# The masked operands of the inverse's levels one to four, made by GpSimd instead of VectorE

## Chip, cores and metric

The kernel runs on one core of a Trainium2 chip. The metric is the device time of one execution in microseconds, the median over several executions. TensorE is PE, its weight loads PEld, VectorE DVE, ScalarE ACT, GpSimd POOL, SyncE SP.

## What is computed

Two sequences of 2048 tokens with 256 channels are normalised. One branch is a recurrent layer (RWKV7 form) with four heads of 64, the other an attention layer with a mixture of four experts; the output is x plus the product of the two. What matters here is the recurrence, a state of 64 x 64 for each sequence and head:

```python
def step(S, inp):
    rt, dt, kt, vt, kkt, at = inp
    sa = jnp.einsum('bhvk,bhk->bhv', S, -kkt)
    S = S * dt[:, :, None, :] + sa[..., None] * (kkt * at)[:, :, None, :] + vt[..., None] * kt[:, :, None, :]
    y = jnp.einsum('bhvk,bhk->bhv', S, rt)
    return (S, y)
...
x = x + s * g          # s: this layer's output; g: silu of the attention and experts branch
```

## The kernel before, in words

Three phases run one after the other: the recurrent phase (up to about 1170 us), the attention, the experts. Only the recurrent phase is touched.

It takes 16 turns t of 128 tokens of both sequences. The steps of the recurrence are done by chunks of 64 tokens (CH), so a turn has 4 chunks of 2 halves of the channels: 8 pairs (PAIRS), each with two heads stacked on the 128 partitions. Within a chunk the feedback through `sa` is a triangular system of 64 x 64, and the kernel inverts it by doubling: `inv` and `invT` start as the inverse of blocks of two (the masks of `base`), and five further levels (`lev` 0 to 4; LEVELS is 6) join blocks of twice the size. A level needs the part of the matrix below its diagonal blocks: `am[:, :, 0, :]`, the first of seven products kept for each pair, times a 0/1 mask `lev`. That is the masked operand `lj`, held in two buffers `lj[0]` and `lj[1]` in turns. Of a level, PE first makes z = inv x lj into bank 4, ACT copies it to `zz`, PE makes invT x zz and zz x invT into banks 5 and 6, and DVE adds these to `inv` and `invT`. At the last level only `invT` is updated.

Each engine's program of a turn interleaves three strands: `back(t)`, the inverse and the chunks of turn t; `front(t)`, the projections and features of the next 128 tokens; `tail(t - 1)`, the group norm and output projection of the turn before. `back` calls `give_way()` at fixed places, and each call runs the other two strands up to their next `yield`. So the order on each engine is fixed by the code; an engine does its rows in order, and the engines meet only in semaphores. A `Signal` counts the steps of a turn: `at(t, n)` is the value at which n of turn t are done. The first turn has no tail and the last no front.

On DVE the row of work at the start of a turn is: r_yc of the tail, the statistics of the next x, eight masked products `am` (L870), after the fourth and after the eighth the five masks of `base` (L857 to L863) on half the pairs, and then the front's dx (L731) and token mixes (L709), whose g is PE's next input (g1). Before the change DVE makes `lj` of level 0 in `base` (L860) and that of levels 1 to 4 at L880, each at the head of the level before its use, ahead of the front and tail work that `give_way` brings. PE waits for `s_lj`, which counts six signals a turn: two of `base`, four of L880. GpSimd has no program in this phase.

Of the kernel before, what the change touches and what calls it, by code (L numbers as in the profile page):

```python
# [8 lines left out]
ALU = mybir.AluOpType  # L9
# [8 lines left out]
NT = T // TT  # L18
# [3 lines left out]
PAIRS = CB * HALVES  # L22
LEVELS = int(math.log2(CH))
# [62 lines left out]
def all_strands(eng, front, back, tail):  # L86


    for _ in front(FIRST):
        pass  # L90

    def turn(t, before, after):
        strands = [tail(t - 1) if before else iter(()), front(t) if after else iter(())]

        def give_way():
            for strand in strands:
                next(strand, None)

        back(t, give_way)
        for strand in strands:  # L100
            for _ in strand:
                raise AssertionError("the strands differ in length")

    turn(0, False, True)
    with eng.Fori(1, NT - 1) as t:
        turn(t, True, True)
    turn(NT - 1, True, False)
    for _ in tail(NT - 1):
        pass


def recurrent_phase(nc, io, keep, signal):
# [13 lines left out]
    with ctx:  # L126
        def sb(name, shape, dt=FP32):
            return ctx.enter_context(nc.sbuf_tensor("r_" + name, shape, dt))

        def sig(name, per, unit=1):  # L130
            return signal("r_" + name, per, unit)
# [8 lines left out]
        def v(name, h):  # L140
            return vec[:, VECS.index(name), h:h + 1]
# [34 lines left out]
        am = sb("am", [128, PAIRS, 7, 64])  # L176
        inv, invT, zz = (sb(n, [128, PAIRS, 64]) for n in ("inv", "invT", "zz"))
        lj = [sb(f"lj{i}", [128, PAIRS, 64]) for i in range(2)]
# [25 lines left out]
        def by_batch(ap):  # L204
# [10 lines left out]
        s_adec, s_vst = sig("a_r_decayed", 1), sig("v_stacked", 1)  # L215
        s_xsq, s_h, s_hsq, s_cut = sig("xn_squared", 1), sig("h", 1), sig("qk_squared", 2), sig("parts", 2)
        s_am, s_amsb = sig("products", PAIRS), sig("products_kept", PAIRS)
        s_lj, (s_z, s_zsb, s_inv, s_invsb) = sig("level_off", LEVELS), (sig(n, LEVELS - 1) for n in (
            "z", "z_kept", "inverse_step", "inverse_kept"))
        s_g, s_gsb, s_u, s_usb, s_sn, s_state, s_y, s_ysb = (sig(n, NCH) for n in (  # L220
            "chunk_g", "chunk_g_kept", "chunk_u", "chunk_u_kept", "state_gain", "state", "chunk_y", "chunk_y_kept"))
# [3 lines left out]
        front_step, back_step, tail_step = sig("dve_front_step", 15), sig("dve_back_step", 5), sig("dve_tail_step", 2)  # L225
        s_base = sig("transposed_base", 2)
# [5 lines left out]
        block = ctx.enter_context(nc.Block())  # L232
# [53 lines left out]
        def _(pe):  # L286
            back_signals, tail_signals = (s_am, s_z, s_inv, s_g, s_u, s_sn, s_y), (s_mean, s_gvar, s_out)
# [117 lines left out]
            def back(t, give_way):  # L405
# [24 lines left out]
                def pairwise(bk, left, right):  # L430
                    apart()
                    for p in range(PAIRS):
                        for j in range(2):
                            q = slice(64 * j, 64 * j + 64)
                            last = mm(ps[q, bk, 64 * p:64 * p + 64], left[q, p, :], right[q, p, :], start=True, stop=True)  # L435
                    return last

                for lev in range(LEVELS - 1):
                    if lev:
                        pe.wait_ge(s_invsb.sem, s_invsb.at(t, lev))  # L440
                    pe.wait_ge(s_lj.sem, s_lj.at(t, lev + 2))
                    pairwise(4, lj[lev % 2], inv).then_inc(s_z.sem, s_z.up())
                    give_way()
                    pe.wait_ge(s_zsb.sem, s_zsb.at(t, lev + 1))
                    if lev == 0:
                        pe.wait_ge(s_base.sem, s_base.at(t, 2))
                    if lev < LEVELS - 2:
                        pairwise(5, invT, zz)
                    pairwise(6, zz, invT).then_inc(s_inv.sem, s_inv.up())
                    give_way()  # L450
# [231 lines left out]

        @block.vector
        def _(dve):
            back_signals = (s_amsb, s_base, s_lj, s_invsb, s_state, back_step)
            tail_signals = (s_yc, s_yg, tail_step)
            for q in back_signals + tail_signals:
                q.open(dve)
# [1 line left out]
            ve = nc.vector  # L690
# [157 lines left out]
            def back(t, give_way):  # L848
                flat = lambda a: a[:, :, :].rearrange("p a c -> p (a c)")
                wide = lambda name, lo=0, hi=64, n=PAIRS: const(name, lo, hi).unsqueeze(1).to_broadcast([128, n, 64])  # L850

                def base(p):


                    n = PAIRS // 2
                    dve.wait_ge(s_amsb.sem, s_amsb.at(t))
                    ve.tensor_tensor(inv[:, p, :], am[:, p, 6, :], wide("low0", n=n), ALU.mult)  # L857
                    ve.tensor_tensor(invT[:, p, :], am[:, p, 0, :], wide("low0t", n=n), ALU.mult
                                     ).then_inc(back_step.sem, back_step.up())
                    ve.tensor_tensor(lj[0][:, p, :], am[:, p, 0, :], wide("lev", 0, 64, n), ALU.mult)  # L860
                    dve.wait_ge(back_step.sem, back_step.at(t))
                    ve.tensor_tensor(inv[:, p, :], inv[:, p, :], wide("eye64", n=n), ALU.add).then_inc(s_lj.sem, s_lj.up())  # L862
                    ve.tensor_tensor(invT[:, p, :], invT[:, p, :], wide("eye64", n=n), ALU.add  # L863
                                     ).then_inc(s_base.sem, s_base.up())


                give_way()
                for p in range(PAIRS):
                    dve.wait_ge(s_am.sem, s_am.at(t, p + 1))
                    ve.tensor_tensor(am[:, p, :, :].rearrange("p a c -> p (a c)"), ps[:, 4 + p % 3, 0:448],  # L870
                                     const("amask"), ALU.mult).then_inc(s_amsb.sem, s_amsb.up())
                    if p == PAIRS // 2 - 1:
                        base(slice(0, PAIRS // 2))
                        give_way()
                base(slice(PAIRS // 2, PAIRS))
                dve.wait_ge(s_base.sem, s_base.at(t))
                give_way()
                for lev in range(LEVELS - 1):
                    if lev < LEVELS - 2:
                        ve.tensor_tensor(lj[(lev + 1) % 2][:, :, :], am[:, :, 0, :], wide("lev", 64 * lev + 64, 64 * lev + 128),  # L880
                                         ALU.mult).then_inc(s_lj.sem, s_lj.up())
                    give_way()
                    dve.wait_ge(s_inv.sem, s_inv.at(t, lev + 1))
                    if lev < LEVELS - 2:
                        ve.tensor_tensor(flat(inv), flat(inv), ps[:, 5, :], ALU.add)  # L885
                    ve.tensor_tensor(flat(invT), flat(invT), ps[:, 6, :], ALU.add).then_inc(s_invsb.sem, s_invsb.up())
                    dve.wait_ge(s_invsb.sem, s_invsb.at(t))
                    if lev == 2:


                        for h in range(2):
                            ve.tensor_scalar(gain[:, h, :], gT[:, h, :], v("ln_w", h), None, ALU.mult)
                            last = ve.scalar_tensor_tensor(shift[:, h, :], bonus[:, h, :], v("ln_b", h), gT[:, h, :],
                                                           ALU.add, ALU.mult)
                        last.then_inc(back_step.sem, back_step.up())
                        dve.wait_ge(back_step.sem, back_step.at(t))
                    give_way()
                for c in range(NCH):
                    fl = lambda a: a[:, :, :, :].rearrange("p b g v -> p (b g v)")
                    give_way()  # L900
                    give_way()

                    dve.wait_ge(s_sn.sem, s_sn.at(t, c + 1))
                    ve.tensor_tensor(fl(stmp), fl(state), ps[:, 6, 0:256], ALU.add).then_inc(back_step.sem, back_step.up())
                    dve.wait_ge(back_step.sem, back_step.at(t))
                    ve.tensor_tensor(state[:, :, :, :], stmp[:, :, :, :],
                                     p_end[:, c, :, :].unsqueeze(3).to_broadcast([128, B, 2, 64]), ALU.mult
                                     ).then_inc(s_state.sem, s_state.up())
                    dve.wait_ge(s_state.sem, s_state.at(t))
                    give_way()  # L910
                back_step.whole()
                for q in back_signals:
                    q.restart()
# [22 lines left out]
                    q.restart()  # L936

            all_strands(dve, front, back, tail)


PARTS_Q, PARTS_K = (0, 0, 0, 1, 1, 2), (0, 1, 2, 0, 1, 0)
# [957 lines left out]
```

## Time and profile before

| what | value |
|---|---|
| median of 3 runs | 3104.87 us (3094.93 to 3106.5) |
| the profiled execution | 3108.72 us, span 3106.9 us |
| PE busy | 2727.6 us, 88% |
| DVE busy | 2074.6 us, 67% |
| ACT busy | 1330.4 us, 43% |
| POOL busy | 63.7 us, 2%, x91 |

The span runs from the first to the last instruction of the profiled execution. Busy shares are means over three phases with different limits; what the change is worth has to be read from the waits and the timeline of the recurrent phase. A number in square brackets behind an instruction is the idle time of its engine before it and the instruction that ended it. A tile's name carries r_ in front for this phase; `cst` holds the masks, `xn_all` the normalised input. A row with x4 or x32 is a run of equal instructions merged, its time that of the whole run.

### The profile page before, as it was taken

What the parts mean: (1) busy time and instruction counts of PE and PEld (TensorE: products, weight loads), DVE (VectorE), ACT (ScalarE), POOL (GpSimd) and SP (SyncE); (2) the same over time, 40 slices, a digit from 0 to 9 for tenths busy, and PEclk for the clock granted to TensorE, in tenths of its full rate; (3) what the DMA queues carried; (4) which work ended last, traced back from release to release, by engine and by line L of the source; (5) the groups of instructions that cost most, each with busy time, mean ns of one, the idle gap of its engine ahead of it and who ended that gap; (6) DMA issues with size and microseconds to landing.
All of it is one profiled execution on the core that took longest, in us unless ns stands there. A gap on an engine that the chain in (4) does not pass through costs nothing. (4 is left out here: it accounts for less than half of the span.)

```text
span 3106.9 us, 71943 instructions
## 1 busy us (share of the span) xinstructions
PE 2727.6 (88%) x27049; PEld 1834.5 (59%) x27049; DVE 2074.6 (67%) x4070; ACT 1330.4 (43%) x1993; POOL 63.7 (2%) x91
## 2 busy tenths in 40 slices
PE   6988888888888876898988989889894999999999
PEld 5767776767777761233323323232333999999999
DVE  6666766776666748776776767667674555655654
ACT  3333333333333410155555555545552554445444
POOL 0000000000000001000000000000004000000000
PEclk9999999999999985699999999999997999999999
DMA  2000000000100003001111010110104010011010
GB/s 65 19 19 19 21 24 23 20 19 19 26 19 19 16 16 98 1 21 36 32 36 45 12 45 23 44 46 11 45 21 132 28 34 27 24 34 32 22 30 24
DMA packets 141929, 96.89 MB, mean 31 GB/s; under 512 B 69088, under 2 KB 137312, under 8 KB 140640
## 3 DMA queue, kind: packets, MB, share of 16 engines
q1 hardware_dynamic: 140064, 87.66, 9.8%
q0 software_dynamic: 1600, 5.24, 0.5%
q8 instruction: 221, 3.62, 0.5%
q14 instruction: 44, 0.36, 0.0%
HBM read 63.18 MB, written 29.36 MB: 30 GB/s over the span
## 5 line engine op out<-in xcount | busy, mean ns | idle before, releaser
L1209 DVE TENSOR_REDUCE a_mx<-a_pm 128x1 f32<-128x512 f32 (+3 forms) x1440 | 812.6, 607 | 280.8 <-PE a_pm L1091 147.0
L1192 ACT ACTIVATE a_pt<-a_sc 128x1024 f32<-128x1024 f32 (+3 forms) x640 | 562.0, 896 | 611.8 <-PE a_sc L1120 426.8
L1088 PE MATMUL a_pm<-a_ka,a_qa 96*128 96x512 bf16 (+3 forms) x1440 | 521.2, 379 | 98.5 <-DVE a_mx L1209 56.5
L1088 PEld LDWEIGHTS a_pm<-a_ka,a_qa 96*128 96x128 bf16 x1440 | 136.4, 98 | 582.3 <-DVE a_mx L1209 511.2
L1120 PE MATMUL a_sc<-a_qa,a_ka 98*128 98x512 bf16 (+3 forms) x1280 | 368.5, 361 | 37.4 <-DMA a_qa<-a_mrow 33.2
L1167 PE MATMUL a_po<-a_pt,a_v_st 128*32 128x512 f32 (+3 forms) x2560 | 305.2, 549 | 0.0
L1759 DVE TENSOR_TENSOR e_h_lo<-v_all,e_h_hi 128x512 fp32r<-128x512 f32 x208 | 145.7, 701 | 189.1 <-ACT e_h_hi L1606 187.9
L1120 PEld LDWEIGHTS a_sc<-a_qa,a_ka 98*128 98x128 bf16 x1280 | 116.7, 100 | 147.5 <-issue 50.3
L1604 ACT ACTIVATE v_all<-e_ps 128x512 f32<-128x512 f32 x176 | 103.6, 589 | 124.2 <-PE e_ps L1496 123.4
L1496 PE MATMUL e_ps<-e_h_hi,e_e_l_hi 128*128 128x256 f32 x512 | 147.7, 288 | 0.0
L1496 PE MATMUL e_ps<-e_h_lo,e_e_l_hi 128*128 128x256 f32 x512 | 144.8, 283 | 0.0
L1496 PE MATMUL e_ps<-e_h_hi,e_e_l_lo 128*128 128x256 f32 x512 | 144.8, 283 | 0.0
L885 DVE TENSOR_TENSOR r_inv<-r_inv,r_ps 128x512 f32<-128x512 f32 x64 | 43.9, 686 | 132.3 <-PE r_ps L435 132.3
L1091 PE MATMUL a_pm<-a_masks 128*128 128x128 bf16 x576 | 131.1, 235 | 0.0
L435 PE MATMUL r_ps<-r_zz,r_invT 64*64 64x64 f32 x2048 | 83.4, 238 | 46.9 <-ACT r_zz L645 46.9
L435 PE MATMUL r_ps<-r_inv,r_lj 64*64 64x64 f32 x2560 | 95.7, 226 | 32.1 <-DVE r_inv L862 27.6
L435 PEld LDWEIGHTS r_ps<-r_inv,r_lj 64*64 64x64 f32 x2560 | 85.0, 139 | 55.9 <-issue 55.9
L435 PEld LDWEIGHTS r_ps<-r_zz,r_invT 64*64 64x64 f32 x2048 | 74.6, 151 | 71.3 <-issue 71.3
L1606 ACT ACTIVATE e_h_hi<-v_all 128x512 fp32r<-128x512 f32 x176 | 111.1, 631 | 5.7
L645 ACT ACTIVATE r_zz<-r_ps 128x512 f32<-128x512 f32 x80 | 47.3, 591 | 141.3 <-PE r_ps L435 141.3
L1123 PE MATMUL a_sc<-a_masks 128*128 128x128 bf16 x512 | 101.4, 219 | 0.0
L1496 PEld LDWEIGHTS e_ps<-e_h_lo,e_e_l_hi 128*128 128x128 f32 x512 | 98.2, 192 | 0.4
(321 smaller groups left out, 5627.4 us busy)
## 6 DMA issues: line engine op xcount, KB each, us to landing
a_qa<-q_scratch SPq DMA_DIRECT2D x240, 64.0 KB, 2.3
a_ka<-k_scratch SPq DMA_DIRECT2D x240, 64.0 KB, 2.3
o_scratch<-a_o_sb SPq DMA_DIRECT2D x8, 1024.0 KB, 5.6
v_all<-o_scratch SPq DMA_DIRECT2D x256, 32.0 KB
q_scratch<-r_q_part SPq DMA_DIRECT2D x192, 32.0 KB, 1.8
k_scratch<-r_k_part SPq DMA_DIRECT2D x192, 32.0 KB, 1.6
r_x_tok<-in_x SPq DMA_DIRECT2D x32, 128.0 KB, 2.1
s_scratch<-r_s_tok SPq DMA_DIRECT2D x32, 128.0 KB, 1.7
```

What stands on the lines that cost most here:

```text
L435: last = mm(ps[q, bk, 64 * p:64 * p + 64], left[q, p, :], right[q, p, :], start=True, stop=True)
L1088: last = mm(out[:, 0:width], qa[b][0:NP, h, 128 * qt:128 * qt + 128], ka[b][0:NP, h, 512 * kc:512 * kc + width], start=True, stop=not diag)
L1091: last = mm(out[:, width - 128:width], ident16, neg_qk, start=False, stop=True)
L1120: last = mm(sc[x][:, y, off:512], ka[b][:, h, 128 * j:128 * j + 128], qa[b][:, h, 512 * qc + off:512 * qc + 512], start=True, stop=not diag)
L1123: last = mm(sc[x][:, y, off:off + 128], ident16, neg_kq, start=False, stop=True)
L1167: last = mm(po[qc % 2][32 * h:32 * h + 32, off:512], v_st[b][:, j, h, :], pt[h // 2][n % 2][:, h % 2, off:512], start=(j == 0), stop=(j == ...
L1192: nc.scalar.activation(pt[x][n % 2][:, :, off:512], sc[x][:, :, off:512], ACT.Exp).then_inc(s_p[x].sem, s_p[x].up())
L1209: return ve.tensor_reduce(mx[:, h, qt, kc:kc + 1], pm[i % 2][:, 0:width], axis=AX.X, op=ALU.max)
L1496: last = mm(out, a, b, start=(n == 0), stop=(n == len(products) - 1))
L1604: f(tmp[m % 2][:, :, :], two, ACT.Gelu).then_inc(by["A"].sem, by["A"].up())
L1606: f(hi[dst][:, o:o + 2, :], tmp[m % 2][:, :, :], ACT.Copy).then_inc(s_hi.sem, s_hi.up())
L1759: ve.tensor_tensor(lo[dst][:, o:o + 2, :], tmp[m % 2][:, :, :], hi[dst][:, o:o + 2, :], ALU.subtract).then_inc(s_lo.sem, s_lo.up())
```

## The change

The four products that make `lj` for levels 1 to 4 leave DVE's program, and GpSimd gets a program of its own in this phase that makes them: level 1 when all eight products `am` of the turn are kept, each further level when PE has done the first product of the level before the one in hand (`s_z`), which frees the buffer. `lj` of level 0 stays with DVE. PE waits for a signal of its own for level 0 (`s_first`) and for GpSimd's (`s_lj`) at the others.

```diff
-        s_lj, (s_z, s_zsb, s_inv, s_invsb) = sig("level_off", LEVELS), (sig(n, LEVELS - 1) for n in (
+        s_first, s_lj, (s_z, s_zsb, s_inv, s_invsb) = sig("base", 2), sig("level_off", LEVELS - 2), (sig(n, LEVELS - 1) for n in (
             "z", "z_kept", "inverse_step", "inverse_kept"))
@@ PE
-                    pe.wait_ge(s_lj.sem, s_lj.at(t, lev + 2))
+                    if lev:
+                        pe.wait_ge(s_lj.sem, s_lj.at(t, lev))
+                    else:
+                        pe.wait_ge(s_first.sem, s_first.at(t, 2))
                     pairwise(4, lj[lev % 2], inv).then_inc(s_z.sem, s_z.up())
@@ DVE, base
-                    ve.tensor_tensor(inv[:, p, :], inv[:, p, :], wide("eye64", n=n), ALU.add).then_inc(s_lj.sem, s_lj.up())
+                    ve.tensor_tensor(inv[:, p, :], inv[:, p, :], wide("eye64", n=n), ALU.add).then_inc(s_first.sem, s_first.up())
@@ DVE, levels
                 for lev in range(LEVELS - 1):
-                    if lev < LEVELS - 2:
-                        ve.tensor_tensor(lj[(lev + 1) % 2][:, :, :], am[:, :, 0, :], wide("lev", 64 * lev + 64, 64 * lev + 128),
-                                         ALU.mult).then_inc(s_lj.sem, s_lj.up())
                     give_way()
@@ new
+        @block.gpsimd
+        def _(pool):
+            s_lj.open(pool)
+
+            def levels(t):
+
+                pool.wait_ge(s_amsb.sem, s_amsb.at(t, PAIRS))
+                for lev in range(LEVELS - 2):
+                    if lev:
+                        pool.wait_ge(s_z.sem, s_z.at(t, lev))
+                    mask = const("lev", 64 * lev + 64, 64 * lev + 128).unsqueeze(1).to_broadcast([128, PAIRS, 64])
+                    nc.gpsimd.tensor_tensor(lj[(lev + 1) % 2][:, :, :], am[:, :, 0, :], mask, ALU.mult
+                                            ).then_inc(s_lj.sem, s_lj.up())
+                s_lj.restart()
+
+            levels(0)
+            with pool.Fori(1, NT - 1) as t:
+                levels(t)
+            levels(NT - 1)
```

On DVE, at the places that the text calls A and B, from the first mask of `base` on the second half of the pairs in the first turn, the row was, before:

```order
L857 TENSOR_TENSOR r_inv<-r_am,cst 128x256
L858 TENSOR_TENSOR r_invT<-r_am,cst 128x256
L860 TENSOR_TENSOR r_lj0<-r_am,cst 128x256
L862 TENSOR_TENSOR r_inv<-r_inv,cst 128x256
L863 TENSOR_TENSOR r_invT<-r_invT,cst 128x256
L731 TENSOR_TENSOR r_dx<-xn_all 128x512
L709 SCALAR_TENSOR_TENSOR r_xg<-r_dx,vec,xn_all 128x256 x2
L709 SCALAR_TENSOR_TENSOR r_xw<-r_dx,vec,xn_all 128x256 x2
L880 TENSOR_TENSOR r_lj1<-r_am,cst 128x512
L709 SCALAR_TENSOR_TENSOR r_xa<-r_dx,vec,xn_all 128x256 x2
```

And after the change (the same instructions have line numbers higher by three):

```order
L860 TENSOR_TENSOR r_inv<-r_am,cst 128x256
L861 TENSOR_TENSOR r_invT<-r_am,cst 128x256
L863 TENSOR_TENSOR r_lj0<-r_am,cst 128x256
L865 TENSOR_TENSOR r_inv<-r_inv,cst 128x256
L866 TENSOR_TENSOR r_invT<-r_invT,cst 128x256
L734 TENSOR_TENSOR r_dx<-xn_all 128x512
L712 SCALAR_TENSOR_TENSOR r_xg<-r_dx,vec,xn_all 128x256 x2
L712 SCALAR_TENSOR_TENSOR r_xw<-r_dx,vec,xn_all 128x256 x2
L712 SCALAR_TENSOR_TENSOR r_xa<-r_dx,vec,xn_all 128x256 x2
```

Only L880's row is gone; everything else keeps its place. On GpSimd, the loop's turn now is (before, this engine had no row in the phase):

```order
L951 TENSOR_TENSOR r_lj1<-r_am,cst 128x512 [waits r_products_kept]
L949 ISA
L951 TENSOR_TENSOR r_lj0<-r_am,cst 128x512 [waits r_z]
L949 REGISTER_ALU
L951 TENSOR_TENSOR r_lj1<-r_am,cst 128x512 [waits r_z]
L949 REGISTER_ALU
L951 TENSOR_TENSOR r_lj0<-r_am,cst 128x512 [waits r_z]
```

Each of the four products has a wait of its own: the first on the event that also lets DVE's masks go, the others on PE's first product of the level before.

## Rows read from the trace of the kernel before

**Rows 1.** First line; then 100 us: PE, PEld, DVE, ACT, POOL busy, granted clock, DMA.
```profile
span 3106.9 us, 71943 instructions
...
600.00:700.00 100.00, 84.91 (x1322) 69.18 (x1318) 72.92 (x159) 34.23 (x68) 0.00 (x0) 1.00 0.10 23
```

**Rows 2.** Waits from 71 to 1140 us: total us, times, longest.
```profile
PE r_ps L435 <- DVE r_inv L862: 25.9, 15, 2.3
...
PE r_ps L313 <- DVE r_xg L709: 12.5, 14, 1.1
```

**Rows 3.** Timeline, turn 8, all engines: start, us, engine, line, operation, idle before.
```profile
619.07 0.42 DVE L857 TENSOR_TENSOR r_inv<-r_am,cst 128x256 f32<-128x256 f32 x1
...
620.09 0.42 DVE L862 TENSOR_TENSOR r_inv<-r_inv,cst 128x256 f32<-128x256 f32 x1
...
620.65 1.15 PE L435 MATMUL r_ps<-r_inv,r_lj 64*64 64x64 f32 x32 [1.69 <-DVE r_inv L862]
621.12 0.69 DVE L731 TENSOR_TENSOR r_dx<-xn_all 128x512 f32 x1 [0.29 <-DVE r_invT L863]
...
621.85 0.88 DVE L709 SCALAR_TENSOR_TENSOR r_xg<-r_dx,vec,xn_all 128x256 f32<-128x256 f32 x2
...
622.87 1.13 PE L313 MATMUL r_ps<-r_xg,r_g 128*128 128x256 f32 x4 [1.07 <-DVE r_xg L709]
623.44 0.69 DVE L880 TENSOR_TENSOR r_lj<-r_am,cst 128x512 f32<-128x512 f32 x1
```

**Rows 4.** The tile r_lj: count, duration in ns (min/median/max).
```profile
L880 DVE TENSOR_TENSOR r_lj<-r_am,cst x64: 680/685/693, 64.4 to 1135.4; 128x512 f32<-128x512 f32 x64
```

**Rows 5.** The same timeline further on, DVE and PE.
```profile
631.62 0.68 DVE L926 TENSOR_TENSOR r_yg<-r_yc,r_ystd 128x512 f32<-128x512 f32 x1
...
633.07 0.69 DVE L930 TENSOR_TENSOR r_yg<-r_yg,r_shift 128x512 f32<-128x512 f32 x1
...
634.02 1.99 PE L520 MATMUL r_ps<-r_W_o,r_yg 128*128 128x256 f32 x8
```

**Rows 6.** Timeline of DVE from 640 us.
```profile
645.78 0.69 DVE L885 TENSOR_TENSOR r_inv<-r_inv,r_ps 128x512 f32<-128x512 f32 x1 [2.22 <-PE r_ps L435]
...
650.04 0.68 DVE L880 TENSOR_TENSOR r_lj<-r_am,cst 128x512 f32<-128x512 f32 x1
```

**Rows 7.** Timeline of PE from 640 us.
```profile
653.58 1.15 PE L435 MATMUL r_ps<-r_zz,r_invT 64*64 64x64 f32 x32 [2.92 <-ACT r_zz L645]
```

**Rows 8.** Line L1301, GpSimd products of two SBUF operands: durations in ns.
```profile
L1301 POOL TENSOR_TENSOR e_l_lo<-a_stage,e_l_hi x2: 1256/1256/1256, 1221.8 to 1224.6; 128x512 fp32r<-128x512 f32 x2
```

**Rows 9.** Timeline from 2377.6 us: DVE back to back, then beside a GpSimd product.
```profile
2377.71 0.69 DVE L1790 TENSOR_TENSOR e_e_down_lo<-v_all,e_e_down_hi 128x512 fp32r<-128x512 f32 x1 [1.29 <-ACT e_e_down_hi L1618]
2378.32 0.69 DVE L1790 TENSOR_TENSOR e_e_l_lo<-v_all,e_e_l_hi 128x512 fp32r<-128x512 f32 x1
...
2379.56 1.58 POOL L1301 TENSOR_TENSOR e_e_l_lo<-v_all,e_e_l_hi 128x512 fp32r<-128x512 f32 x1
...
2379.95 2.35 DVE L1790 TENSOR_TENSOR e_e_l_lo<-v_all,e_e_l_hi 128x512 fp32r<-128x512 f32 x2
...
2381.62 0.68 DVE L1790 TENSOR_TENSOR e_e_l_lo<-v_all,e_e_l_hi 128x512 fp32r<-128x512 f32 x1
```

**Rows 10.** Timeline of DVE: r_yc (L918) opens each turn; four of them.
```profile
116.71 0.69 DVE L918 SCALAR_TENSOR_TENSOR r_yc<-r_ps,r_yT 128x512 f32<-128x512 f32 x1 [0.22 <-PE r_ps L507]
...
609.82 0.69 DVE L918 SCALAR_TENSOR_TENSOR r_yc<-r_ps,r_yT 128x512 f32<-128x512 f32 x1 [1.99 <-PE r_ps L507]
...
678.02 0.69 DVE L918 SCALAR_TENSOR_TENSOR r_yc<-r_ps,r_yT 128x512 f32<-128x512 f32 x1 [1.94 <-PE r_ps L507]
...
1102.93 0.69 DVE L918 SCALAR_TENSOR_TENSOR r_yc<-r_ps,r_yT 128x512 f32<-128x512 f32 x1 [0.21 <-PE r_ps L507]
```

**Rows 11.** Timeline of PE: the g1 group in two other turns.
```profile
129.61 1.80 PE L313 MATMUL r_ps<-r_xg,r_g 128*128 128x256 f32 x4 [1.08 <-DVE r_xg L709]
...
978.75 2.07 PE L313 MATMUL r_ps<-r_xg,r_g 128*128 128x256 f32 x4 [0.25 <-DVE r_xg L709]
```

More of the change, by code:

```diff
@@ L684, in _ @@
         def _(dve):
-            back_signals = (s_amsb, s_base, s_lj, s_invsb, s_state, back_step)
+            back_signals = (s_amsb, s_base, s_first, s_invsb, s_state, back_step)
             tail_signals = (s_yc, s_yg, tail_step)
```

## The prediction

> **What bounds the kernel now.** I read the busy time first, then the waits of TensorE (PE), then the timeline around each wait. In a stretch of 100 us in the recurrent phase PE is busy 84.91 us and VectorE (DVE) 72.92 us, and GpSimd (POOL) does nothing [rows 1]. So DVE's busy time is not the limit by itself: what it does costs time only where PE, or somebody PE waits for, stands behind it. The operand that moves, r_lj, never makes PE wait. The waits of PE that name DVE in this phase are 25.9 us on r_inv from L862 (15 times) and 12.5 us on the mixed operand r_xg from L709 (14 times) [rows 2]. Both lie within four microseconds at the start of the inverse, once in each turn. In turn 8 DVE ends the last of eight products r_am at about 619.0, starts the base masks at 619.07, and starts L862 at 620.09; PE, idle for 1.69 us, starts the first product r_ps<-r_inv,r_lj at 620.65. It is idle again for 1.07 us until r_xg is there, and starts the g1 projection at 622.87 [rows 3]. I call these places A and B. From 622.87 the timeline shows PE occupied almost without a break until it waits 2.92 us, up to 653.58, for ScalarE's r_zz [rows 7]; I call that C. The chain to C begins with PE itself: DVE waits 2.22 us for PE's products at 645.78, updates the inverse, and some steps later hands ScalarE the norms that its row of work before r_zz needs.
>
> **What is removed, and what it is worth.** DVE loses four products a turn, 64 in all, 685 ns each [rows 4], 64 x 0.685 = 43.8 us of busy time. I look at what follows each of them.
> Level 1 (623.44) stands behind r_xg and r_xw, so A and B end before it [rows 3]. What follows it are r_xa and r_xk, which PE reaches only behind g1, w1 and the second half of the level before: worth nothing.
> Level 2 stands ahead of the three products that make r_yg for the output projection. From its start, 631.01, to the start of the next, 631.62, are 0.61 us; r_yg ends at 633.07 + 0.69 = 633.76, and PE's L520 starts at 634.02 directly behind its group before [rows 5]. r_yg was already in time by 0.26 us: worth nothing.
> Level 3 is followed by DVE's wait for PE of 2.22 us [rows 6]: worth nothing.
> Level 4 (650.04) comes after the norm that ScalarE waits for, and in front of a step that waits for ScalarE [rows 6]: worth nothing to C.
> So the work removed is hidden today by PE's own work, and if that cover were gone a level would be worth 0.61 us.
>
> **What is added.** GpSimd makes the same four products. No row shows it doing so in this phase. The nearest rows are its products of two SBUF operands of 128x512 further on, 1256 ns with nothing beside them [rows 8]; I take 1.26 us. Here one operand is read in eight pieces of 64 and the other is repeated eight times. If GpSimd has to be told of each piece, it might be twice that, 2.5 us, which I take as the upper bound; the lower is DVE's own 0.685 us. The result is in time in either case: level 1 is made after the eighth r_am and read after PE's whole row of groups from 622.87, and each later level is made one level ahead.
>
> What it costs others is the point. The row to look at is where GpSimd's product runs beside DVE products of two SBUF operands. Back to back these start 0.61 us apart, at 2377.71 and 2378.32. One that starts at 2379.95, while GpSimd's is under way from 2379.56 for 1.58 us, holds its successor off until 2381.62, so 1.67 us: 1.06 us lost, and the DVE product ends about when GpSimd's has ended plus its own work [rows 9]. GpSimd's product is itself longer than 1.26 by 0.32. They take turns. The base masks (L857 to L863), r_dx (L731) and the mixes (L709) all read two operands in SBUF; the updates of the inverse and r_am read one of theirs from PSUM, and I take these as free of it.
> The Trainium skill speaks against the change here: "SBUF — State Buffer", section "Who interferes with whom", says that a DVE instruction with two SBUF inputs and a GpSimd one that reads SBUF exclude each other for the whole instruction. By that rule each meeting would cost the full 1.26 us and the sum below would be 45 us without the clock, where the row gives 36. The same skill's "GPSIMD Engine Reference", section "Elementwise — side-by-side cycle accounting", has 4497 ns for 2048 elements; a quarter is an estimate of 1.12 us, and with 0.92 lost at a meeting the sum would be about 31 us.
>
> **The sum.**
> A: GpSimd's level 1 is released by the eighth r_am, the very event that releases DVE's five masks from 619.07. Even if DVE starts first, GpSimd comes between two of the five, and L862 is the fourth. 1.06 us later r_inv, and PE waits 2.75 instead of 1.69: 16 turns x 1.06 = 17.0 us.
> B: level 2 is released by PE's first product, which ends 1.15 us after its start, when DVE is at the two halves of r_xg (before: 620.65 + 1.15 = 621.80, and r_xg from 621.85 [rows 3]; both move by the same 1.06). One half waits again, or, if GpSimd is a little late, r_xw, which PE wants next. I take the full price: 15 turns with a next block of inputs x 1.06 = 15.9 us; the other bound is 0.
> Level 3 is released when PE's second level product ends, about 631.0, as DVE starts r_yg, now 0.61 us earlier. 1.06 - 0.61 = 0.45 late, less 0.26 in hand: 0.19 x 15 = 2.9 us.
> Level 4 falls before DVE's idle 2.22 us, which has grown by 0.61: nothing.
> PE does not make up what A and B cost, since C hangs on PE's own products. Together 17.0 + 15.9 + 2.9 = 35.8 us.
> The clock: in turn 8 the g1 group takes 1.13 us at the high level; in 8 of the 14 turns that follow the first it takes 1.7 to 2.07, the first and last being those at 129.61 and 978.75 [rows 3, 11], so TensorE was granted 1.2 instead of 2.4 GHz there, each time behind the idle time at A. The price of all such stretches, C's too: the 14 turns from 116.71 to 1102.93 take 70.44 us on average, turn 8 without one 678.02 - 609.82 = 68.20 [rows 10], so 2.24 x 14 = 31.4 us. With twice the idle time at A and B I expect the low level in all 15 turns, 7 more. If A's turns carry all of that price it is 31.4 / 8 = 3.9 each, 27 us; but the longer idle time itself covers part of a slow stretch, in the 8 turns too, so the lower bound is 0. I take 5, nearer the low end for that reason.
> Sum: 35.8 + 5 = about 41 us. The profiled execution took 3108.7 us (span 3106.9), the median of the runs is 3104.9, so it stands 3.9 above. On the median: **about 3146 us**, 1.3% slower.
>
> **Rivals.** A measurement tells 0.5%, 15.5 us, from no change.
> First, only one of the two meetings costs PE, because GpSimd starts late enough to fall in DVE's wait of 0.29 us before r_dx, or behind r_xg: one time 17 us, 3122. For it: no row shows how soon GpSimd starts after another engine's signal. Against: DVE's products stand without a gap for 1.8 us there.
> Second, no change: DVE and GpSimd run side by side here and the 64 products were hidden anyway: 3105. For it: the rows of the meeting are few and from another phase. Against: it is the same kind of instruction, same size.
> Third, faster: the delay at A moves the turn's idle times, and the stretches at the low clock become rarer. If they vanished, the stage would go to 68.20 a turn, 31 us less: 3074. It decides if at least half of the slow stretches go (15.7 us) while the meetings cost nothing; against it, more idle time stands ahead of the place where the clock is low already.
> Fourth, GpSimd's product takes 2.5 us: a meeting costs 2.5 - 0.2 = 2.3, so A 36.8, B 34.5, level 3 (2.3 - 0.61 - 0.26) x 15 = 21.5, together 93, 3198.
>
> **How the numbers follow.** Forecast 0.66 (its own range 3128 to 3166: from two thirds of the 35.8 with no clock term to all of it with 25 for the clock), first rival 0.13, no change 0.10, faster 0.05, fourth 0.06. A range from 3112 to 3182 leaves out the second and third rivals and most of the fourth, 0.2. Slower by over 0.5%: the forecast, the fourth and 0.09 of the first, 0.81; within 0.5%: 0.10 and the other 0.04, 0.14; faster 0.05.
>
> **What would show it.** In the changed profile: POOL products r_lj of about 1.26 us, some longer by 0.3; a mask of L860 to L865 and an r_xg that take near 1.5 us instead of 0.42; PE's wait on r_inv about 2.75 and on r_xg about 2.1; nothing waits for r_lj; g1 at the low clock in nearly all turns; later phases as before. It would be wrong if the masks keep 0.42 us, or if PE's waits at A and B are unchanged.

## The result, and the profile after

The changed kernel takes 3133.62 us (median of 4 runs, 3123.18 to 3143.25), beside 3104.73 us before in the same comparison: 1.0099 times the time, 95% interval 1.006 to 1.0138. It is 28.9 us slower; the forecast was 41 slower. The profiled execution is the shortest of the four, 3123.18 us, so its trace has about half of the median's loss in it.

The busy time of the changed kernel in a stretch of 100 us, with the columns of [rows 1]:

```profile
600.00:700.00 100.00, 87.02 (x1404) 71.18 (x1404) 70.46 (x147) 35.47 (x71) 6.17 (x4) 0.97 0.10 23
```

GpSimd is busy 6.17 us there and the granted clock is 0.97 of full speed, where [rows 1] show 0 and 1.00.

The waits of PE from 71 to 1140 us (total us, times, longest), to be held against [rows 2]:

```profile
PE r_ps L435 <- DVE r_inv L865: 42.0, 15, 3.4
...
PE r_ps L313 <- DVE r_xg L712: 3.5, 14, 0.3
PEld r_ps L523 <- DVE r_yg L930: 2.9, 14, 0.2
```

The wait on r_inv has grown from 25.9 to 42.0 us, and the wait on r_xg has shrunk from 12.5 to 3.5. A wait of the weight loads on r_yg is new, 2.9 us in 14 turns. Nothing in this list waits for r_lj.

The timeline of the changed kernel at places A and B in one turn, which answers to [rows 3]:

```profile
631.00 0.42 DVE L860 TENSOR_TENSOR r_inv<-r_am,cst 128x256 f32<-128x256 f32 x1
...
631.04 1.51 POOL L951 TENSOR_TENSOR r_lj<-r_am,cst 128x512 f32<-128x512 f32 x1 [45.80 <-DVE r_am L873]
631.34 1.49 DVE L861 TENSOR_TENSOR r_invT<-r_am,cst 128x256 f32<-128x256 f32 x1
...
633.65 1.98 PE L435 MATMUL r_ps<-r_inv,r_lj 64*64 64x64 f32 x32 [2.76 <-DVE r_inv L865]
...
634.85 0.88 DVE L712 SCALAR_TENSOR_TENSOR r_xg<-r_dx,vec,xn_all 128x256 f32<-128x256 f32 x2
635.65 1.89 DVE L712 SCALAR_TENSOR_TENSOR r_xw<-r_dx,vec,xn_all 128x256 f32<-128x256 f32 x2
...
635.70 1.55 POOL L951 TENSOR_TENSOR r_lj<-r_am,cst 128x512 f32<-128x512 f32 x1 [3.15 <-PE r_ps L435]
...
635.86 2.07 PE L313 MATMUL r_ps<-r_xg,r_g 128*128 128x256 f32 x4 [0.24 <-DVE r_xg L712]
```

The first mask and GpSimd's level 1 start 0.04 us apart, on the same event. The second mask, L861, takes 1.49 us where it took 0.42. PE waits 2.76 us, and its first product r_ps<-r_inv,r_lj takes 1.98 us in place of 1.15: the clock is low. So GpSimd's level 2, released by that product, starts at 635.70, when both halves of r_xg (from 634.85) are done, and it meets r_xw, 1.89 us for two halves in place of 0.88. PE starts g1 after a wait of 0.24 us.

GpSimd's products as a group (ns, minimum/median/maximum), to be held against [rows 4, 8]:

```profile
L951 POOL TENSOR_TENSOR r_lj<-r_am,cst x64: 1265/1508/1724, 60.9 to 1148.1; 128x512 f32<-128x512 f32 x64
```

It takes 1.26 or 1.27 us in three of the four products of the last turn, and 1.40 to 1.72 in all full turns, where a VectorE product of two SBUF operands is under way when it starts. 1.27 is the time of a product of plain rows [rows 8], so the eight strided pieces and the repeated mask cost nothing.

The same timeline at r_yg, which answers to [rows 5]:

```profile
645.71 0.69 DVE L926 TENSOR_TENSOR r_yg<-r_yc,r_ystd 128x512 f32<-128x512 f32 x1
...
645.82 1.72 POOL L951 TENSOR_TENSOR r_lj<-r_am,cst 128x512 f32<-128x512 f32 x1 [8.57 <-PE r_ps L435]
646.44 1.64 DVE L928 TENSOR_TENSOR r_yg<-r_yg,r_gain 128x512 f32<-128x512 f32 x1
...
648.11 0.69 DVE L930 TENSOR_TENSOR r_yg<-r_yg,r_shift 128x512 f32<-128x512 f32 x1
```

The second of the three products that make r_yg, L928, takes 1.64 us (1.64 or 1.65 in each of the 14 turns), and the three end 3.09 us after their start, beside 2.14 before.

The first and the last full turn, by r_yc, as in [rows 10]:

```profile
120.30 0.69 DVE L918 SCALAR_TENSOR_TENSOR r_yc<-r_ps,r_yT 128x512 f32<-128x512 f32 x1 [0.23 <-PE r_ps L510]
...
1120.93 0.69 DVE L918 SCALAR_TENSOR_TENSOR r_yc<-r_ps,r_yT 128x512 f32<-128x512 f32 x1 [0.21 <-PE r_ps L510]
```

1120.93 - 120.30 = 1000.63 us for 14 turns, 71.47 a turn, where the kernel before had 70.44.

### The profile page after: what moved, and what is told of

The parts are those of the page before. It is cut to its first block and busy times, and to the rows that moved or that the text cites. A ratio compares the mean times of both kernels' runs of the same rounds, so it can differ in the third digit from the quotient of the medians.

```text
span 3121.3 us, 72087 instructions
## 1 busy us (share of the span) xinstructions
PE 2736.2 (88%) x27049; PEld 1836.5 (59%) x27049; DVE 2099.0 (67%) x4006; ACT 1330.7 (43%) x1993; POOL 161.4 (5%) x155
## 5 line engine op out<-in xcount | busy, mean ns | idle before, releaser
L951 POOL TENSOR_TENSOR r_lj<-r_am,cst 128x512 f32<-128x512 f32 x64 | 97.5, 1524 | 1051.4 <-DVE r_am L873 736.1
L435 PE MATMUL r_ps<-r_inv,r_lj 64*64 64x64 f32 x2560 | 105.0, 240 | 49.4 <-DVE r_inv L865 44.7
L435 PEld LDWEIGHTS r_ps<-r_inv,r_lj 64*64 64x64 f32 x2560 | 93.8, 152 | 73.2 <-issue 73.2
L435 PE MATMUL r_ps<-r_zz,r_invT 64*64 64x64 f32 x2048 | 76.4, 226 | 46.8 <-ACT r_zz L648 46.8
L435 PEld LDWEIGHTS r_ps<-r_zz,r_invT 64*64 64x64 f32 x2048 | 68.0, 139 | 72.9 <-issue 72.9
```

## Experiments

Each was compared with runs of the kernel before on the same chip. There were three such groups: the first four experiments, beside 3099.2 us; B by itself, the VectorE delay, and the changed kernel and the kernel before with TensorE kept busy, beside 3101.8; and the other three, beside 3102.9. The theory is that of the prediction: what is saved is hidden, and GpSimd's reading holds VectorE off at A and B. The first rival: the loss lies elsewhere, in lost VectorE time or in the new signals.

### Nobody makes the operands

```diff
-                    pairwise(4, lj[lev % 2], inv).then_inc(s_z.sem, s_z.up())
+                    pairwise(4, lj[0], inv).then_inc(s_z.sem, s_z.up())
...
-        @block.gpsimd
```

> Nobody makes the masked operands of levels 1 to 4: VectorE's four products are gone and GpSimd has no program; every level reads the operand of level 0, so the output is not the reference's. It measures what the removal alone is worth. My theory (removed work is hidden by TensorE's own work): no change against the kernel before, 3105 within 8 us; TensorE's wait on r_inv at place A stays 1.69 us and the wait of 2.92 us at C stays. Rival (the saved VectorE work is worth something and the meetings at A ate it): 64 x 0.61 us at most, down to 3066, some 10 us faster or more.

Measured: 3096.3 us, 0.9986 (0.997 to 1.0002). Its waits of PE:

```profile
PE r_ps L435 <- ACT r_zz L646: 46.0, 18, 2.9
...
PE r_ps L435 <- DVE r_inv L863: 25.9, 15, 2.3
```

The wait on r_inv is the 25.9 us of [rows 2], and C's 2.9 is there. 43.8 us of VectorE's work removed give back 2.8 us in the median and at most 0.3%, 9 us, by the interval, which also reaches no change. The removed work was hidden. (The output is not the reference's, since every level reads the operand of level 0.)

### GpSimd's products added, VectorE's kept

```diff
+        def _(pool):
...
+                    nc.gpsimd.tensor_tensor(kT[:, :, :, :].rearrange("p h c d -> p (h c) d"), am[:, :, 0, :], mask, ALU.mult).then_inc(s_spare.sem, s_spare.up())
```

> The kernel before, with VectorE still making every masked operand, and GpSimd making the same four products a turn besides, at the same moments as in the changed kernel, into a buffer that is unused at that time. My theory (the cost is GpSimd's reading beside VectorE's products): as the changed kernel or a little more, 3125 to 3150, with the second mask of base at about 1.5 us instead of 0.42 and the wait on r_inv at 2.76. Rival (the cost is in how PE's waits and the two signals are arranged, not in GpSimd's reading): 3105.

Measured: 3146.0 us, 1.0137 (1.0109 to 1.0165). Its waits:

```profile
PE r_ps L435 <- DVE r_inv L864: 38.6, 14, 2.8
...
PE r_ps L313 <- DVE r_xg L709: 13.1, 14, 2.1
...
PE r_ps L520 <- DVE r_yg L932: 11.2, 14, 0.8
```

The cost comes with GpSimd's products; TensorE's signals are those of before (VectorE has one more wait a turn, before it writes the buffer that GpSimd uses). At 46.9 us it is 18 larger than in the changed kernel, and two waits say why. VectorE still has 0.61 us a level in front of r_yg, which now makes PE itself wait 11.2 us. And the wait on r_xg is 13.1 us in place of 3.5: in 5 of the 14 full turns PE's first product runs at 1.15 to 1.30 us though the wait in front of it was 2.76, and PE waits 1.93 to 2.08 us at B as well. In one of them:

```profile
571.81 1.15 PE L435 MATMUL r_ps<-r_inv,r_lj 64*64 64x64 f32 x32 [2.76 <-DVE r_inv L864]
...
573.02 1.89 DVE L709 SCALAR_TENSOR_TENSOR r_xg<-r_dx,vec,xn_all 128x256 f32<-128x256 f32 x2
573.13 1.49 POOL L954 TENSOR_TENSOR r_kT<-r_am,cst 128x512 f32<-128x512 f32 x1 [2.42 <-PE r_ps L435]
...
575.03 2.07 PE L313 MATMUL r_ps<-r_xg,r_g 128*128 128x256 f32 x4 [2.08 <-DVE r_xg L709]
```

### GpSimd writes only

```diff
+                    nc.gpsimd.memset(kT[:, :, :, :], 0.0)
+                    nc.gpsimd.memset(bT[:, :, :, :], 0.0).then_inc(s_spare.sem, s_spare.up())
```

> As the run before, but GpSimd only writes zeros (two memsets of 128x512 in place of each product) and reads nothing from SBUF. My theory (only the reading of two engines excludes each other): no stretched mask at A, the wait on r_inv at 1.69, 3105 within 8 us. Rival (any GpSimd work on SBUF holds VectorE off): the mask that meets the memsets grows by 0.4 to 0.9 us, and the time goes to 3115 or more.

Measured: 3097.6 us, 0.9986 (0.9964 to 1.0007). The timeline at A:

```profile
336.87 0.53 POOL L954 MEMSET r_kT<- 128x512 f32 x1 [46.39 <-DVE r_am L872]
337.10 0.42 DVE L860 TENSOR_TENSOR r_invT<-r_am,cst 128x256 f32<-128x256 f32 x1
...
338.33 1.15 PE L435 MATMUL r_ps<-r_inv,r_lj 64*64 64x64 f32 x32 [1.69 <-DVE r_inv L864]
```

The memsets, 0.53 us each, lie beside the masks, the second mask keeps 0.42 us (in every turn), PE waits 1.69. So it is the reading that is exclusive, as "SBUF — State Buffer", section "Who interferes with whom", of the Trainium skill says of a VectorE instruction with two SBUF inputs; the trace agrees.

### The products released later

```diff
-                pool.wait_ge(s_amsb.sem, s_amsb.at(t, PAIRS))
                 for lev in range(LEVELS - 2):
-                    if lev:
-                        pool.wait_ge(s_z.sem, s_z.at(t, lev))
+                    pool.wait_ge(s_z.sem, s_z.at(t, max(lev, 1)))
+                    if more and lev < 2:
+                        pool.wait_ge(s_mix.sem, s_mix.at(t, 2))
+                    if more and lev == 2:
+                        pool.wait_ge(s_cs.sem, s_cs.at(t, 1))
```

In the code `more` is false in the last turn, which has no next block of inputs.

> The changed kernel with GpSimd's products released later: levels 1 and 2 after r_xw and the first product of level 0, level 3 after the decay sums, level 4 as it was. Nothing meets the masks of base. My theory: the wait at A returns to 1.69 us, TensorE's clock falls at A no more often than in the kernel before, and the time returns to 3105 within 10 us; the products now meet r_xa and r_xk, which have more than 1 us in hand. Rival (GpSimd's products cost wherever they lie, through the lost VectorE time): stays at 3120 to 3135.

Measured: 3099.0 us, 1.0003 (0.9981 to 1.0025). Waits, and the timeline where levels 1 and 2 now lie:

```profile
PE r_ps L435 <- DVE r_inv L865: 25.9, 15, 2.3
...
PE r_ps L313 <- DVE r_xg L712: 13.3, 14, 1.1
```

```profile
407.67 1.12 PE L313 MATMUL r_ps<-r_xg,r_g 128*128 128x256 f32 x4 [1.07 <-DVE r_xg L712]
408.25 1.89 DVE L712 SCALAR_TENSOR_TENSOR r_xa<-r_dx,vec,xn_all 128x256 f32<-128x256 f32 x2
408.41 2.85 POOL L953 TENSOR_TENSOR r_lj<-r_am,cst 128x512 f32<-128x512 f32 x2 [49.68 <-DVE r_xw L712]
```

The two products (2.85 us together) meet r_xa, which takes 1.89 us in place of 0.88, and nothing waits for it. The GpSimd work is the same. VectorE is busy 2084.0 us over the whole execution, beside 2099.0 in the changed kernel and 2038.0 where nobody makes the operands, so about 46 us of its time are still lost, where the changed kernel lost about 61, and they cost nothing: the rival of lost VectorE time is out. What counts is where the meeting lies.

### B by itself

```diff
+                    if not lev:
+                        ve.tensor_tensor(lj[1][:, :, :], am[:, :, 0, :], wide("lev", 64, 128), ALU.mult
+                                         ).then_inc(s_first.sem, s_first.up())
...
-                for lev in range(LEVELS - 2):
+                for lev in range(1, LEVELS - 2):
```

> The changed kernel with level 1 given back to VectorE (at its old place) and levels 2 to 4 left to GpSimd. So nothing meets the masks of base (A), and GpSimd's level 2 starts when TensorE's first product ends, as in the changed kernel. It prices place B of the prediction by itself. The prediction's step (level 2 meets a half of r_xg at the high clock and PE waits 2.1 us there): 15 turns x 1.06 = 16 us and some for the clock, 3115 to 3125. Rival, from the profile of the changed kernel (GpSimd starts after both halves of r_xg and meets r_xw, which PE needs only behind g1): 3 to 8 us, 3103 to 3108; the wait on r_xg stays 1.07 in turns at the high clock.

Measured: 3136.7 us, 1.0109 (1.0077 to 1.014), more than either theory gave. Waits, and a turn's A and B:

```profile
PE r_ps L313 <- DVE r_xg L712: 27.7, 14, 2.2
```

```profile
632.68 1.15 PE L435 MATMUL r_ps<-r_inv,r_lj 64*64 64x64 f32 x32 [1.69 <-DVE r_inv L865]
...
633.88 1.97 DVE L712 SCALAR_TENSOR_TENSOR r_xg<-r_dx,vec,xn_all 128x256 f32<-128x256 f32 x2
633.91 1.26 POOL L952 TENSOR_TENSOR r_lj<-r_am,cst 128x512 f32<-128x512 f32 x1 [49.78 <-PE r_ps L435]
...
635.98 1.50 PE L313 MATMUL r_ps<-r_xg,r_g 128*128 128x256 f32 x4 [2.15 <-DVE r_xg L712]
```

A is as it was: 1.69 us, and the product behind it runs at the high clock, 1.15 us. So GpSimd's level 2 starts at 633.91, 0.03 us behind r_xg, which takes 1.97 us; PE waits 2.15. That is the prediction's step B (1.07 + 1.06 = 2.13). The rival read from the changed profile was wrong: in 13 of the 14 full turns the first product takes 1.15 to 1.28 us and PE waits 1.95 to 2.15 at B. Beyond the 15 x 1.08 = 16 us and about 3 of r_yg, whose wait of the weight loads is 3.0 us here too, 16 are left. The clock is the likely part: behind the longer wait it falls in every such turn, at the latest in w1, the group behind g1 (g1 at 1.50 us here in place of 1.13, w1 at 1.81 to 1.97 in place of 1.08).

### A by itself: VectorE delayed without GpSimd

```diff
+                    if p.start:
...
+                        ve.tensor_tensor(idle, cst[:, 0:512], cst[:, 512:1024], ALU.mult)
...
+                        ve.tensor_tensor(idle[:, 0:384], cst[:, 0:384], cst[:, 512:896], ALU.mult)
```

> The kernel before, without GpSimd, with two idle VectorE products (512 and 384 elements wide, into buffers unused at that time) put between the second and third mask of base on the second half of the pairs: a delay of about 1.07 us at A and nowhere else. My theory (all of the change's cost is this delay at A and the clock that falls behind the longer wait): the time of the changed kernel, 3122 to 3136, the wait on r_inv at 2.76 and the low clock in every turn. Rival (a large part is paid by the other meetings, with r_xw, r_yg and r_xsq): 3112 to 3118.

Measured: 3125.7 us, 1.0076 (1.0051 to 1.0101), 23.9 us. The timeline of a turn:

```profile
631.94 0.68 DVE L862 TENSOR_TENSOR r_kT<-cst 128x512 f32<-128x512 f32 x1
...
632.54 0.55 DVE L864 TENSOR_TENSOR r_bT<-cst 128x384 f32<-128x384 f32 x1
...
633.90 1.97 PE L435 MATMUL r_ps<-r_inv,r_lj 64*64 64x64 f32 x32 [2.75 <-DVE r_inv L867]
...
636.12 2.07 PE L313 MATMUL r_ps<-r_xg,r_g 128*128 128x256 f32 x4 [0.25 <-DVE r_xg L709]
```

A delay of 1.07 us on VectorE, with no GpSimd in the phase, gives A's wait of 2.75, the low clock on the first product (1.97) and the short wait at B (0.25): the pattern of the changed kernel, and most of its loss. In one of the 14 full turns, though, the first product runs at 1.15 us behind the same wait, and in another at 1.55.

### A by itself: only level 1 on GpSimd

```diff
-                for lev in range(LEVELS - 2):
+                for lev in range(1):
...
+                    if 0 < lev < LEVELS - 2:
+                        ve.tensor_tensor(lj[(lev + 1) % 2][:, :, :], am[:, :, 0, :], wide("lev", 64 * lev + 64, 64 * lev + 128),
+                                         ALU.mult).then_inc(s_first.sem, s_first.up())
```

> Only level 1 is made by GpSimd, released as in the changed kernel by the eighth product; levels 2 to 4 are VectorE's at their old places. It prices place A alone, as the run with level 1 given back to VectorE priced place B alone. My theory now (A pushes TensorE's clock to its low level, the first product of the inverse takes 1.97 us, and B costs nothing any more): the wait on r_inv at 2.76 us, low clock in every turn, about the cost of the VectorE delay, 3120 to 3133. Rival (the other meetings of the changed kernel, with r_xw, r_yg and r_xsq, carry a good part): under 3118.

Measured: 3135.6 us, 1.0097 (1.0067 to 1.0127), range 3121.8 to 3143.4. Its waits, whose profiled execution was the longest, 3143.35 us:

```profile
PE r_ps L435 <- DVE r_inv L865: 38.6, 14, 2.8
...
PE r_ps L313 <- DVE r_xg L712: 8.1, 14, 1.1
```

One of the four products, at A, costs as much as all four, 1.0099. The median lies 2.6 us above what was expected, and 10 above the VectorE delay's, whose interval overlaps with this one. The expectation of the low clock in every turn behind A failed in part: in 6 of the 14 full turns the first product runs at 1.15 to 1.29 us behind the wait of 2.76, PE then waits 0.93 to 1.07 at B, and the clock falls in g1 instead (2.07 us). In 7 of 15 turns it is low behind C as well (r_ps<-r_zz,r_invT at 1.38 to 1.97 us).

### The changed kernel with TensorE kept busy

```diff
+                def keep_busy(n):
+
+                    for k in range(n):
+                        mm(ps[:, 6, 0:256], ident, cst[:, 0:256], start=True, stop=True)
+
+                pe.wait_ge(s_amsb.sem, s_amsb.at(t, 6))
+                keep_busy(5)
                 for lev in range(LEVELS - 1):
...
+                    if lev == 3:
+                        keep_busy(8)
                     pe.wait_ge(s_zsb.sem, s_zsb.at(t, lev + 1))
```

An idle matmul here is one whose result nobody reads; it only fills a wait of TensorE.

> The changed kernel with idle matmuls (128x256, into a bank that is free at that time) put where TensorE waits: five before the wait on r_inv at A, eight before the wait on r_zz at level 3 (C). They need nothing that is not there and fit into the wait. If the low clock is what costs beside the direct 1.06 us a turn, it stays at 2.4 GHz and a turn takes 68.2 + 1.1 to 70 us instead of 71.5: 3095 to 3115. Rival (the clock does not follow TensorE's idle time at A, or the low stretch is hidden): 3125 to 3150, slower by what the matmuls take from PE.

Measured: 3141.3 us, 1.0123 (1.0095 to 1.0152), where 3095 to 3115 was expected. The timeline of a turn:

```profile
1001.67 1.03 PE L441 MATMUL r_ps<-cst 128*128 128x256 f32 x4
...
1003.30 1.15 PE L435 MATMUL r_ps<-r_inv,r_lj 64*64 64x64 f32 x32 [0.60 <-DVE r_inv L874]
...
1004.51 1.96 DVE L721 SCALAR_TENSOR_TENSOR r_xg<-r_dx,vec,xn_all 128x256 f32<-128x256 f32 x2
1004.54 1.26 POOL L960 TENSOR_TENSOR r_lj<-r_am,cst 128x512 f32<-128x512 f32 x1 [2.33 <-PE r_ps L435]
...
1006.61 1.43 PE L313 MATMUL r_ps<-r_xg,r_g 128*128 128x256 f32 x4 [2.15 <-DVE r_xg L721]
```

The idle matmuls (the last of them in the first row) hold the clock at A, and the first product takes 1.15 us. But then GpSimd's level 2 starts at 1004.54 on top of r_xg, PE waits 2.15 us at B, and the clock falls there (g1 1.43). It is so in all 14 full turns: first product 1.15, wait at B 2.15. With A's low clock taken away, B's price comes back. So it is the low clock of the first product that keeps B free.

### The kernel before with TensorE kept busy

The same idle matmuls in the kernel before.

> The kernel before with the same idle matmuls. If the clock is the price it was taken for, every turn takes the 68.2 us of turn 8: about 30 us less than before, 3065 to 3080. Rival (the matmuls cost what they give, or the clock is not governed by this): 3095 to 3110.

Measured: 3080.9 us, 0.9929 (0.99 to 0.9957), 21 us less, at the upper edge of what was expected. PE in a turn, and the stretch of [rows 1]:

```profile
606.87 2.32 PE L441 MATMUL r_ps<-cst 128*128 128x256 f32 x10
609.12 1.15 PE L435 MATMUL r_ps<-r_inv,r_lj 64*64 64x64 f32 x32
610.94 1.12 PE L313 MATMUL r_ps<-r_xg,r_g 128*128 128x256 f32 x4 [0.66 <-DVE r_xg L718]
```

```profile
600.00:700.00 100.00, 94.71 (x1341) 77.49 (x1336) 74.80 (x160) 38.44 (x73) 0.00 (x0) 1.00 0.08 21
```

The five idle matmuls (two records each, so x10) take 2.32 us, more than the 1.69 us of wait at A, so that the first product starts later and the wait at B shrinks from 1.07 to 0.66 us. The granted clock is 1.00, and g1 takes 1.12 or 1.13 us in all full turns. 21 us are what the idle matmuls give back. What the low clock had cost is at least about that, since they also start the first product later.

### Both, with the products released later

The later release, with the idle matmuls.

> GpSimd's products released later (levels 1 and 2 after r_xw, level 3 after the decay sums) and the idle matmuls at A and C. If the removed VectorE work is worth nothing also where TensorE's clock stays high, this is the time of the kernel before with idle matmuls, 3076 to 3086. Rival (with the clock high VectorE is nearer the path and its 2.4 us a turn count): 3060 to 3073. Other rival (GpSimd's products meet something that has no time in hand at the high clock): over 3090.

Measured: 3079.3 us, 0.9924 (0.9897 to 0.9952). As the kernel before with idle matmuls: VectorE's 64 products are worth nothing that can be measured at the high clock either. Both versions beat both kernels, and what they gain is the clock.

### The delay with TensorE kept busy

The VectorE delay at A, with the idle matmuls.

> The kernel before with the idle matmuls at A and C and VectorE's delay of 1.07 us at A. It prices the direct delay with the clock held: 16 x 1.07 = 17 us over the run of the kernel before with idle matmuls (3081), so 3094 to 3102, if the matmuls hold the clock also over the longer wait. With the clock free the same delay cost 24 us. Rival (the wait of about 1.3 us that is left at A still lowers the clock): 3105 or more.

Measured: 3097.7 us, 0.9977 (0.9957 to 0.9996). PE in a turn:

```profile
972.46 1.15 PE L435 MATMUL r_ps<-r_inv,r_lj 64*64 64x64 f32 x32 [0.60 <-DVE r_inv L876]
974.69 1.13 PE L313 MATMUL r_ps<-r_xg,r_g 128*128 128x256 f32 x4 [1.07 <-DVE r_xg L718]
```

3097.7 - 3080.9 = 16.8 us, beside 16 x 1.07 = 17.1: the direct price of the delay at A. The two runs stand in different groups; each against its own kernel before, they are 15.7 apart. The idle matmuls leave 0.60 us at A, B stays at 1.07, and both groups run at the high clock in this turn. They don't hold it everywhere: in 4 of the 14 full turns g1 takes 1.57 to 1.99 us, so some clock is in the 16.8 too. With the clock free the same delay cost 23.9. By that 7 or 8 us of it is clock, but the intervals of these runs are 6 to 9 us wide to either side, and the difference isn't clear of them.

## Why the prediction was right, and where not

**The saved work is worth nothing** that can be told from no change: shown twice, by the kernel in which nobody makes the operands (0.9986) and by the late release with and without idle matmuls.

**A, 17.0 us**: right in mechanism and size. The wait is 2.76 us, the forecast 2.75; in the other direction, moving the meeting away brings 1.69 back and the time with it. The pair with idle matmuls measures it at about 16 us.

**B, 15.9 us**: this is the step that failed in the sum, "I take the full price". The mechanism is right, but only while the first product runs at 1.15 us; alone it costs more than forecast, 34.9 us with its clock and r_yg. In the changed profile the clock is low behind A's longer wait in all 14 full turns, the product takes 1.97 us, GpSimd starts after r_xg, and B costs nothing: waits on r_xg fell from 12.5 to 3.5 us. The prediction had priced the low clock and the meeting apart, and had not seen that the first moves the second. One of its own rows held the sign: in the turn at 978.75 the wait at B is 0.25 us in place of 1.07 [rows 11], and the product in front of it, in the kernel before, is this one:

```profile
976.53 1.97 PE L435 MATMUL r_ps<-r_inv,r_lj 64*64 64x64 f32 x32 [1.69 <-DVE r_inv L862]
```

So the reading that the clock had fallen "each time behind the idle time at A" was too coarse. Of the 8 slow turns the first product is slow in 3; in the other 5 it takes 1.15 us and the clock falls at B, in g1. The bound of 0 for B is what the changed kernel's profile shows, but that is the shortest of its four executions. Since GpSimd's added products and level 1 by itself each have turns with the first product at the high clock behind the same wait, a longer execution may pay for some of B; no profile of one was taken.

**r_yg, 2.9 us**: the new wait of the weight loads is 2.9 us in 14 turns. The mechanism is right; that the digit agrees is luck, since it is the small rest of a difference (1.06 - 0.61 - 0.26 us a turn). Level 4's product meets r_xsq, which takes 1.90 us for two halves at 655.66 in place of 0.88, and no wait of PE that names VectorE grows by it; its price wasn't measured by itself.

**The clock, 5 us**: its place is right, its size not settled. In the changed profile it falls behind A in every turn with a front (r_ps<-r_inv,r_lj at 1.97 us in all 14 full turns). Its price is 7 us by 23.9 - 16.8, with an uncertainty as large. In the profiled execution a turn above 68.20 [rows 10] is 3.27 us longer, 1.07 of it A, 0.2 r_yg and 2.0 clock, and before it was 2.24 of clock: no more than before. A's low stretch has become the rule, and those behind C are gone. There, the products r_ps<-r_zz,r_invT take 1.15 us in 14 of 15 turns of the changed profile (1.42 in the first), and 1.47 to 1.98 in 6 of 15 of the profile before. The spread between executions (20 us in the changed kernel) probably lies in such stretches too, which would be why the profiled loss, 14.5 us, is half the median's; no second profile of the kernel shows it.

**The sum** then is A 17 + r_yg 3 + clock 7 = 27 us, beside 28.9 measured, without B. The forecast of 41 had 15.9 us of B in it that the profile doesn't show, so that the time came inside the forecast's own range (3128 to 3166) is in part luck: its terms without B give 25 us, 3130. Of the rivals, the first (3122, only one of the two meetings costs) named the right case and gave the wrong reason: GpSimd is not late by its own start, 0.04 us behind VectorE, but because PE's product is slow. Doubled GpSimd products, no change and a rarer low clock are out. One aside of the prediction was added up wrongly: with 0.92 us lost at a meeting its terms give 14.7 + 13.8 + 0.8 = 29 us, not about 31.

**Left open**: why the first product runs at the low clock behind a wait of 2.76 us in all full turns of one profile and in only 7 or 8 of 14 in two others; how much of the median's loss is clock; why one product at A costs as much in the median as all four (3135.6 and 3133.6), and 10 us more than the delay without GpSimd, whose interval overlaps. Whether the masks of `base` could be ordered so that GpSimd gets in behind L862 wasn't tried.

## What to carry to other kernels

Work moved from VectorE to GpSimd is to be placed, not only counted: each GpSimd product of 128x512 here took about 1.0 to 1.1 us from the VectorE product with two SBUF operands that it met, and was free where that one had time in hand. Here the event that released GpSimd and VectorE together put the meeting exactly on the work that TensorE waits for, and a later event took the cost away. And before pricing two meetings in a row, ask whether the first changes when the second happens. Where TensorE waits in short pieces, idle matmuls in the wait gave more here (21 us) than all the VectorE work was worth (2.8 us in the median, at most 9).

## What the runs showed of the hardware that was not expected

GpSimd gets in between two queued VectorE products: it starts 0.04 us behind the first and the second is held, although both were ready (L860 0.42, L861 1.49 us). A GpSimd product of eight strided pieces with a repeated operand takes 1.27 us, as one of plain rows [rows 8]. Two short idle times of TensorE with a product of 1.15 us between them (1.69 and 1.07 us) were enough to lower its clock in 5 turns of the kernel before. Behind 2.76 us it was low at once in every full turn of the changed profile, but in only 7 of 14 with GpSimd's products added and 8 of 14 with level 1 alone on GpSimd. In the kernel before, five and eight idle matmuls in the waits kept it at 1.00 over the stretch shown.
